# Last attention: GpSimd instead of VectorE multiplies the turned outputs by their reciprocal sums, and VectorE turns them back three heads later

## The chip, the cores and the metric

The kernel runs on one core of one Trainium2 chip. The metric is the device time of one execution, in microseconds. Engines: TensorE (PE; PEld its weight loads), VectorE (DVE), ScalarE (ACT), GpSimd (POOL), and SyncE (SP), which here only issues DMAs.

## What is computed

Four layers of attention and feed-forward blocks on 4096 tokens of 128 features. The change is in the attention of the last layer, which runs on B = 16 sequences of S = 256 tokens with 16 heads of 8 features:

```python
qkv = (x @ w_qkv.T + b_qkv).reshape(B, S, 3, H, hd)
q, k, v = (qkv[:, :, 0], qkv[:, :, 1], qkv[:, :, 2])
energy = jnp.linalg.norm(q, axis=-1)
mask = (energy > energy.mean() * SPARSITY_THRESHOLD).astype(x.dtype)
scores = jnp.einsum('bihd,bjhd->bijh', q, k) / jnp.sqrt(jnp.float32(hd))
scores = scores * mask[:, :, None, :]
probs = jax.nn.softmax(scores, axis=2)
context = jnp.einsum('bijh,bjhd->bihd', probs, v).reshape(B, S, D)
return context @ w_out.T + b_out
```

To this the expert outputs of the last feed-forward block and the residual are added.

## The kernel before

The whole model is one program with stages. The last stage is this attention; it handles the NB = 16 sequences one by one (called batches n below), each with 16 heads and S = 256 positions. Order within an engine is the order in which the code emits instructions; between engines, semaphores order the work. Every signal (`at_mx`, `at_rz` and so on) counts up and is waited for at a value.

For a batch, the steps are:

1. GpSimd splits q and k into three bf16 parts each (`build_pool`: ten dependent operations of 128x256), five batches ahead. SyncE writes the parts to a DRAM tensor `d_pt` (`parts_sp`, 2 DMAs) and loads them back as stacked rows (`set_sp`, 12 DMAs), four batches ahead.
2. TensorE forms scores (`score_pe`), two batches ahead, and VectorE reduces them to row maxima (`maxima_dve`, one reduction of 128x512 per head). Three PSUM banks hold scores, so TensorE is at most three heads ahead of VectorE.
3. GpSimd negates and splits the maxima (`maxparts_pool`), TensorE turns them (`maxrows_pe`), ScalarE copies them, SyncE sends them to the rows behind q (`maxrows_sp`).
4. TensorE forms the scores again, turned and less their maxima (`weights_pe`), ScalarE takes the exponential, TensorE multiplies with the values and a column of ones (`values_pe`, in groups of four heads), so that each head's sum stands beside its output, in PSUM bank 6, half a batch (8 heads) at a time.
5. Per half `hf`, VectorE turns this bank in blocks of 32x32 (`turned_dve`, 128x512), takes the reciprocals of the sums (`sums_dve`, 128x16) and multiplies the outputs with them (`normed_dve`, 128x128 into half of CX). When both halves are there, it turns CX back into CT (`back_dve`, 128x256).
6. TensorE applies `w_out` to CT and adds the gathered expert outputs (`out_pe`), VectorE adds bias and residual (`added_out_dve`), SyncE stores.

What order the engines keep in iteration n of the loops:

- VectorE (`attend_dve`): behind head h's reduction of batch n+2 stand: h = 4 `turned_dve` of (n-1, 1), h = 5 its `sums_dve`, h = 6 its `normed_dve`, h = 7 `back_dve` of n-1, h = 12 `turned_dve` of (n, 0), h = 13 its `sums_dve`, h = 14 its `normed_dve` and `added_out_dve` of n-1.
- TensorE (`attend_pe`): per head the weights of batch n and the scores of n+2; values every fourth head in two parts; at h = 5 `maxrows_pe` of n+1; at h = 12 `out_pe` of n-1, which waits for `back_dve` of n-1.
- GpSimd (`attend_pool`): `maxparts_pool` of n+1, which waits for all maxima of that batch, the copy of the values of n, two gathers, `build_pool` of n+5 while n+5 < 16.
- SyncE (`attend_sp`): `set_sp` of n+4, which waits until the parts have landed in DRAM, `parts_sp` of n+5, `maxrows_sp` of n+2, `store_sp` of n-1.

Most instructions are emitted in helpers, so that their line is the helper's: L204 matmul (`mm`), L217 tensor_tensor (`tt`), L221 tensor_scalar, L225 scalar_tensor_tensor, L231 reduction, L234 copy or cast. L2770 and L2789 are VectorE's turns, L2774 its reciprocal, L2602 `set_sp`, L2589 `parts_sp`, L2606 `maxrows_sp`, L2653 the gathers.

## Time and profile before

| | |
|---|---|
| median of 3 executions | 2154.72 us (2152.58 to 2161.21) |
| profiled execution | 2164.62 us, span 2162.3 us |
| mean granted clock of TensorE | 0.892 |

```profile
span 2162.3 us, 35614 instructions
## 1 busy us (share of the span) xinstructions
PE 1835.7 (85%) x12446; PEld 1206.0 (56%) x12446; DVE 1277.8 (59%) x4360; ACT 979.1 (45%) x2521; POOL 343.0 (16%) x582
## 2 busy tenths in 40 slices
PE   6888588888787999999998888987899854999888
PEld 5455455555555578874556666553544642963333
DVE  3687688888886445764333767160212332469986
ACT  2423466666665223334442332643453213537656
POOL 0000100000000002310000020004053034307642
PEclk9899699999997687989998568988899966979989
```

The first part gives each engine's busy time. The second cuts the span into 40 slices of 54 us; a digit is the busy share in tenths, and PEclk is the clock that TensorE was granted, in tenths of full speed (1.0 is 2.4 GHz, 0.5 is 1.2 GHz). The last attention fills the last four and a half slices.

### The profile page before, as it was taken

What the parts mean: (1) busy time and instruction counts of PE and PEld (TensorE: products, weight loads), DVE (VectorE), ACT (ScalarE), POOL (GpSimd) and SP (SyncE); (2) the same over time, 40 slices, a digit from 0 to 9 for tenths busy, and PEclk for the clock granted to TensorE, in tenths of its full rate; (3) what the DMA queues carried; (4) which work ended last, traced back from release to release, by engine and by line L of the source; (5) the groups of instructions that cost most, each with busy time, mean ns of one, the idle gap of its engine ahead of it and who ended that gap; (6) DMA issues with size and microseconds to landing.
All of it is one profiled execution on the core that took longest, in us unless ns stands there. A gap on an engine that the chain in (4) does not pass through costs nothing.

```text
span 2162.3 us, 35614 instructions
## 1 busy us (share of the span) xinstructions
PE 1835.7 (85%) x12446; PEld 1206.0 (56%) x12446; DVE 1277.8 (59%) x4360; ACT 979.1 (45%) x2521; POOL 343.0 (16%) x582
## 2 busy tenths in 40 slices
PE   6888588888787999999998888987899854999888
PEld 5455455555555578874556666553544642963333
DVE  3687688888886445764333767160212332469986
ACT  2423466666665223334442332643453213537656
POOL 0000100000000002310000020004053034307642
PEclk9899699999997687989998568988899966979989
DMA  3000200000000000000001100021023102606662
GB/s 116 1 13 13 51 26 27 26 22 25 26 27 35 0 1 2 3 2 0 1 0 79 42 1 1 1 88 36 6 22 56 78 24 71 115 25 101 104 103 39
DMA packets 93280, 76.10 MB, mean 35 GB/s; under 512 B 22320, under 2 KB 85168, under 8 KB 92336
## 3 DMA queue, kind: packets, MB, share of 16 engines
q1 hardware_dynamic: 85424, 65.31, 12.9%
q0 software_dynamic: 7680, 8.53, 2.2%
q8 instruction: 101, 1.65, 0.3%
q14 instruction: 75, 0.61, 0.1%
HBM read 48.86 MB, written 23.51 MB: 33 GB/s over the span
## 4 chain that ended last, share of the span: by engine, by line
PE 54%; DVE 27%; issue 6%; DMA 4%; SPq 3%; ACT 2%; another core or an unknown queue 1%; POOL 1%; DVEq 0%; PEld 0%; PEldq 0%; ACTq 0%; POOLq 0%
PE ps L204 50%; DVE sm L225 6%; DVE wt L225 5%; DVE big L217 3%; DMA d_pt<-big 3%; PE ps L208 2%; PE ps L2515 2%; SPq L2602 1%; DVE tmp L221 1%; DVE big L231 1%; SPq L909 1%; DVE big L225 1%; DVE sm L231 1%; DVE sm L221 1%
## 5 line engine op out<-in xcount | busy, mean ns | idle before, releaser
L213 ACT ACTIVATE tmp<-ps,bi 128x512 f32<-128x512 f32 (+1 forms) x226 | 153.6, 683 | 197.4 <-PE ps L204 183.6
L204 PE MATMUL ps<-big,mw 128*128 128x512 f32 (+3 forms) x476 | 217.9, 553 | 10.0 <-DVEq L252 5.6
L213 ACT ACTIVATE sm<-sm,wt 128x1 f32<-128x1 f32 x480 | 165.0, 344 | 78.8 <-DVE sm L225 50.7
L204 PE MATMUL ps<-big,co 128*128 128x256 f32 (+1 forms) x360 | 140.9, 509 | 62.8 <-ACT big L213 42.3
L213 ACT ACTIVATE big<-ps 128x512 f32<-128x512 f32 (+1 forms) x296 | 150.5, 558 | 77.4 <-PE ps L204 75.2
L231 DVE TENSOR_REDUCE big<-ps 128x2 f32<-128x512 f32 x256 | 160.5, 672 | 17.5 <-PE ps L204 16.5
L204 PEld LDWEIGHTS ps<-ke,big 32*128 32x128 f32 (+2 forms) x1632 | 126.6, 190 | 62.6 <-ACT big L212 46.4
L204 PE MATMUL ps<-ke,big 32*128 32x128 f32 (+2 forms) x1632 | 147.9, 291 | 13.1 <-ACT big L212 2.0
L204 PE MATMUL ps<-ke 48*128 48x256 bf16 (+4 forms) x638 | 126.1, 312 | 31.5 <-DVE big L217 15.4
L204 PE MATMUL ps<-big,tmp 128*32 128x256 f32 (+2 forms) x1180 | 123.5, 407 | 22.2 <-DVE tmp L221 16.7
L204 PE MATMUL ps<-tmp,mw 128*128 128x512 f32 x288 | 140.4, 599 | 0.7 <-ACT tmp L212 0.7
L212 ACT ACTIVATE big<-ps 128x256 f32<-128x256 f32 (+4 forms) x244 | 90.2, 379 | 105.3 <-PE ps L204 89.1
L204 PE MATMUL ps<-big 128*32 128x128 f32 (+5 forms) x898 | 128.5, 297 | 10.2 <-DVE big L231 4.4
L204 PEld LDWEIGHTS ps<-co,sm 128*128 128x128 f32 (+1 forms) x708 | 98.4, 213 | 63.9 <-DVE sm L333 38.4
L204 PE MATMUL ps<-big,wt 128*128 128x512 f32 x208 | 112.6, 644 | 22.3 <-DVEq L252 14.3
L204 PE MATMUL ps<-co,sm 128*128 128x128 f32 (+1 forms) x708 | 110.3, 307 | 23.2 <-DVE sm L333 14.1
L204 PEld LDWEIGHTS ps<-big,co 128*128 128x128 f32 x360 | 64.5, 203 | 93.8 <-ACT big L213 54.3
L204 PEld LDWEIGHTS ps<-big,mw 128*128 128x128 f32 (+1 forms) x476 | 80.8, 199 | 61.7 <-issue 37.3
L234 POOL COPY mw<-mw 128x64 f32<-128x64 f32 x64 | 16.4, 256 | 612.0 <-DMA mw<-d_tab 610.0
L204 PEld LDWEIGHTS ps<-ke 128*128 128x128 f32 (+3 forms) x638 | 64.4, 131 | 86.6 <-DVE big L217 24.2
L204 PE MATMUL ps<-tmp,wt 128*128 128x512 f32 (+1 forms) x212 | 102.0, 571 | 12.5 <-issue 7.8
L212 ACT ACTIVATE tmp<-ps 128x128 f32<-128x128 f32 (+2 forms) x177 | 61.9, 362 | 89.4 <-PE ps L204 52.7
(267 smaller groups left out, 3785.7 us busy)
## 6 DMA issues: line engine op xcount, KB each, us to landing
mw<-d_tab SPq DMA_DIRECT2D x32, 328.0 KB, 3.5
mw<-m SPq DMA_DIRECT2D x2, 4096.0 KB, 12.7
d_pt<-big SPq DMA_DIRECT2D x32, 192.0 KB
ke<-d_pt SPq DMA_DIRECT2D x72, 64.0 KB
big<-d_pt SPq DMA_DIRECT2D x72, 64.0 KB
mw<-d_pt SPq DMA_DIRECT2D x48, 64.0 KB
d_xs<-big SPq DMA_DIRECT2D x1, 2560.0 KB, 14.7
big<-d_xs SPq DMA_DIRECT2D x5, 512.0 KB, 6.4
```

What stands on the lines that cost most here:

```text
L204: return e.matmul(out, lhsT, rhs, start=start, stop=stop)
L208: return e.transpose(out, a, K("ident")[0:n, 0:n])
L212: return e.activation(out, in_, f, scale=scale, **kw)
L213: return e.activation(out, in_, f, bias=0.0 if bias is None else bias, scale=scale, **kw)
L217: return e.tensor_tensor(out, a, b, op)
L221: return e.tensor_scalar(out, a, s1, None, op0)
L225: return e.scalar_tensor_tensor(out=out, in0=a, scalar=s, in1=b, op0=op0, op1=op1)
L231: return e.tensor_reduce(out, a, AX, op)
L234: return e.tensor_copy(out, a)
L909: e.dma_start(BIG[2 + hh][q, :].rearrange("p (c x) -> p c x", x=256)[:, :, 64 * (b % 4):64 * (b % 4) + 64], EKT[q, 16 * hh:16 * hh + 16, : ...
L2515: p = e.matmul(o, TMP[:, 2 + i % 2, 128 * j:128 * j + 128], MW[:, bass.ds(x * 512 + (4096 + 128 * j), 128)], start=False, stop=(j == 3))
L2602: e.dma_start(st_[j][r0 + 8 * t:r0 + 8 * t + 8], d_pt[n, j, part].rearrange("(h d) n -> d h n", d=8)).then_inc(s_st[n % 4], 16)
```

## The change

The product of the turned outputs with the reciprocal sums is no longer formed by VectorE (`normed_dve`) but by GpSimd (`normed_pool`). In GpSimd's loop it stands behind `build_pool` of n+5: first the second half of batch n-1, then the first half of batch n; the second half of the last batch stands behind the loop. VectorE's `back_dve` moves from behind head 7 to behind head 10 and waits for GpSimd's products (`at_nm`). `turned_dve` waits for the product of the same half of the batch before, since it overwrites what that reads; `normed_pool` waits for the turn back of the batch before (`at_ct`), since it overwrites CX.

```diff
--- before.py
+++ after.py
@@ -2563,9 +2563,9 @@
         s_pw, s_mr = ([sem(f"d_{n_}{i}") for i in range(2)] for n_ in ("pw", "mr"))
         s_st, s_gy = ([sem(f"d_{n_}{i}") for i in range(4)] for n_ in ("st", "gy"))
         s_o = sem("d_o")
-        at_parts, at_v, at_m3 = signals("gpsimd", 32, 16, 16)
+        at_parts, at_v, at_m3, at_nm = signals("gpsimd", 32, 16, 16, 32)
         at_ms, at_mt, at_s, at_y, at_o = signals("tensor", 256, 16, 256, 128, 16)
-        at_mx, at_t, at_rz, at_ct, at_x, at_one = signals("vector", 256, 32, 48, 16, 16, 1)
+        at_mx, at_t, at_rz, at_ct, at_x, at_one = signals("vector", 256, 32, 32, 16, 16, 1)
         at_ex, at_m3c = signals("scalar", 256, 16)
         QROW = (0, 0, 0, 1, 1, 2)
         KROW = (0, 1, 2, 0, 1, 0)
@@ -2654,6 +2654,10 @@
                                          bass.IndirectOffsetOnAxis(ap=IXP[:, k:k + 1], axis=0)).then_inc(s_gy[n % 4], 16)
                 if n + 5 < NB:
                     build_pool(e, gn, n + 5)
+                if n:
+                    normed_pool(e, n - 1, 1)
+                normed_pool(e, n, 0)
+            normed_pool(e, NB - 1, 1)
 
 
         def mbank(m):
@@ -2767,6 +2771,8 @@
 
         def turned_dve(e, n, hf):
             e.wait_ge(*at_y(8 * n + 4 * hf + 4))
+            if n:
+                e.wait_ge(*at_nm(2 * n + hf - 1))
             e.transpose(TMP[:, hf, :], PS[:, 6, :]).then_inc(at_t.sem, 1)
 
         def sums_dve(e, n, hf):
@@ -2774,16 +2780,16 @@
             e.reciprocal(ZR[:, 16 * hf:16 * hf + 16].rearrange("p (x b) -> p x b", x=2),
                          TMP[:, hf, :].rearrange("p (x b d) -> p x b d", x=2, d=32)[:, :, :, 8]).then_inc(at_rz.sem, 1)
 
-        def normed_dve(e, n, hf):
-            e.wait_ge(*at_rz(3 * n + hf + 1))
-            p = tt(e, CX.rearrange("p (b x d) -> p x b d", x=4, d=8)[:, 2 * hf:2 * hf + 2],
-                   TMP[:, hf, :].rearrange("p (x b d) -> p x b d", x=2, d=32)[:, :, :, 0:8],
-                   ZR[:, 16 * hf:16 * hf + 16].rearrange("p (x b d) -> p x b d", x=2, d=1).broadcast_to((128, 2, 8, 8)), MU)
-            if hf:
-                p.then_inc(at_rz.sem, 1)
+        def normed_pool(e, n, hf):
+            if n:
+                e.wait_ge(*at_ct(n))
+            e.wait_ge(*at_rz(2 * n + hf + 1))
+            tt(e, CX.rearrange("p (b x d) -> p x b d", x=4, d=8)[:, 2 * hf:2 * hf + 2],
+               TMP[:, hf, :].rearrange("p (x b d) -> p x b d", x=2, d=32)[:, :, :, 0:8],
+               ZR[:, 16 * hf:16 * hf + 16].rearrange("p (x b d) -> p x b d", x=2, d=1).broadcast_to((128, 2, 8, 8)), MU).then_inc(at_nm.sem, 1)
 
         def back_dve(e, n):
-            e.wait_ge(*at_rz(3 * n + 3))
+            e.wait_ge(*at_nm(2 * n + 2))
             if n:
                 e.wait_ge(*at_o(n))
             e.transpose(CT, CX).then_inc(at_ct.sem, 1)
@@ -2806,21 +2812,16 @@
                         turned_dve(e, n, 0)
                     if h == 13:
                         sums_dve(e, n, 0)
-                    if h == 14:
-                        normed_dve(e, n, 0)
                     if h == 4 and n:
                         turned_dve(e, n - 1, 1)
                     if h == 5 and n:
                         sums_dve(e, n - 1, 1)
-                    if h == 6 and n:
-                        normed_dve(e, n - 1, 1)
-                    if h == 7 and n:
+                    if h == 10 and n:
                         back_dve(e, n - 1)
                     if h == 14 and n:
                         added_out_dve(e, n - 1)
             turned_dve(e, NB - 1, 1)
             sums_dve(e, NB - 1, 1)
-            normed_dve(e, NB - 1, 1)
             back_dve(e, NB - 1)
             added_out_dve(e, NB - 1)
```

## Rows read from the trace of the kernel before

**Rows 1.** Timeline of GpSimd, iteration 2: start us, length us, instructions, idle before and its releaser.

```profile
1967.71 0.29 POOL L221 TENSOR_SCALAR big<-big 128x32 f32<-128x32 f32 x1 [2.57 <-DVE big L231]
...
1977.56 0.40 POOL L234 CAST big<-big 128x256 bf16<-128x256 f32 x1
1980.47 0.29 POOL L221 TENSOR_SCALAR big<-big 128x32 f32<-128x32 f32 x1 [2.51 <-DVE big L231]
```

**Rows 2.** Table by stretch, from one start of `maxparts_pool` to the next.

```profile
1954.86:1967.71 12.85, 11.55 (x138) 4.84 (x138) 12.47 (x25) 9.23 (x19) 8.80 (x20) 1.00 0.60 92
1967.71:1980.47 12.76, 11.65 (x138) 4.90 (x137) 12.38 (x25) 8.90 (x19) 8.78 (x19) 1.00 0.66 106
2061.81:2078.87 17.06, 13.76 (x140) 5.53 (x140) 12.58 (x24) 8.88 (x17) 8.91 (x19) 0.80 0.60 92
2092.60:2109.60 17.00, 14.79 (x156) 5.95 (x158) 12.67 (x25) 9.86 (x19) 3.73 (x10) 0.80 0.59 109
2109.60:2122.18 12.58, 11.66 (x138) 4.91 (x140) 12.20 (x25) 8.90 (x18) 3.72 (x10) 1.00 0.51 69
2122.18:2134.75 12.57, 11.87 (x138) 5.20 (x142) 12.11 (x24) 8.78 (x18) 3.72 (x9) 1.00 0.09 24
```

**Rows 3.** Groups of GpSimd by line and shape, last attention: count, busy us, mean ns.

```profile
L217 POOL TENSOR_TENSOR big<-big 128x256 f32<-128x256 f32 x44 | 29.6, 673 | 3.5
...
L217 POOL TENSOR_TENSOR big<-big 128x32 f32<-128x32 f32 x32 | 7.8, 244 | 2.7
```

**Rows 4.** Timeline of VectorE, the same iteration.

```profile
1972.35 0.46 DVE L217 TENSOR_TENSOR tmp<-tmp,big 128x128 f32<-128x128 f32 x1
1972.74 0.68 DVE L231 TENSOR_REDUCE big<-ps 128x2 f32<-128x512 f32 x1
1973.34 0.43 DVE L2789 STREAM_TRANSPOSE tmp<-tmp 128x256 f32<-128x256 f32 x1
1973.69 3.04 DVE L231 TENSOR_REDUCE big<-ps 128x2 f32<-128x512 f32 x5
1976.66 0.69 DVE L2770 STREAM_TRANSPOSE tmp<-ps 128x512 f32<-128x512 f32 x1
1977.73 0.69 DVE L231 TENSOR_REDUCE big<-ps 128x2 f32<-128x512 f32 x1 [0.38 <-PE ps L204]
...
1979.04 0.27 DVE L217 TENSOR_TENSOR tmp<-tmp,big 128x128 f32<-128x128 f32 x1
1979.24 0.48 DVE L225 SCALAR_TENSOR_TENSOR big<-ps,bi,big 128x256 f32<-128x256 f32 x1
1979.63 1.87 DVE L231 TENSOR_REDUCE big<-ps 128x2 f32<-128x512 f32 x3
```

**Rows 5.** Timeline of TensorE, the same iteration: output product and the next weights.

```profile
1976.18 0.70 PE L204 MATMUL ps<-tmp,wt 128*128 128x256 f32 x2
...
1977.26 0.28 PE L204 MATMUL ps<-big 51*128 51x256 bf16 x1
```

**Rows 6.** Timeline of VectorE at the end of the kernel.

```profile
2157.61 0.29 DVE L217 TENSOR_TENSOR tmp<-tmp,big 128x128 f32<-128x128 f32 x1
2157.93 0.45 DVE L2789 STREAM_TRANSPOSE tmp<-tmp 128x256 f32<-128x256 f32 x1
```

**Rows 7.** Timeline of TensorE: the two longest waits for a transfer.

```profile
2063.30 0.39 PE L204 MATMUL ps<-big 51*128 51x256 bf16 x1 [3.30 <-DMA big<-big]
...
2094.10 0.39 PE L204 MATMUL ps<-mw 51*128 51x256 bf16 x1 [3.31 <-DMA mw<-big]
```

**Rows 8.** Table by stretch, TensorE alone: us, busy, clock, DMA share, GB/s.

```profile
2064.00:2066.00 2.00, 2.00 (x20) 0.50 0.65 88
```

**Rows 9.** SyncE: its longest total wait (us, times, longest), and issues of set loads.

```profile
SPq L2602 <- DMA d_pt<-big: 48.8, 11, 5.6
...
2047.34 4.64 SPq L2602 DMA_DIRECT2D mw<-d_pt  x12
...
2062.84 4.56 SPq L2602 DMA_DIRECT2D ke<-d_pt  x12
```

## The prediction

> **What bounds the kernel now.** I read the page first for the span, 2162.3 us, then the timeline of GpSimd for the rhythm of the last attention, because GpSimd's first negation of a batch (`maxparts_pool`) starts only when VectorE has finished a batch of row maxima, so each of its starts marks the start of a new iteration n [rows 1]. Call that start P(n). The table by iteration, cut at these starts, has P(1) = 1954.86, P(11) = 2092.60, P(12) = 2109.60 and P(14) = 2134.75 [rows 2]. Thirteen iterations therefore take 179.9 us of the 2162.3.
>
> The same table shows two regimes [rows 2]. In the undisturbed one an iteration takes 12.76 us and VectorE is busy for 12.38 of them; the last full iterations, in which GpSimd builds no parts any more, take 12.58. VectorE sets this pace: 16 reductions at 0.59 us, two turns, two reciprocals, two products, a turn back and a sum. In the other regime (the rows of 17.06 and 17.00 us) VectorE is busy for no more than 12.7 us, and the granted clock drops. The cause is in the timeline of TensorE: it stands for 3.30 us for the DMA of the maxima rows, and starts again at half clock, 0.50; a second stand of this kind, 3.31 us, opens the iteration at 2092.60 [rows 7, 8]. That DMA is queued on SyncE behind the loads and stores of the parts, and SyncE itself waits 48.8 us in 11 waits for the parts to land [rows 9]. So from P(6) or so to P(11) the chain of transfers and not VectorE sets the pace, while before P(6) and after P(12) it is VectorE.
>
> GpSimd is the relaxed engine. In one iteration its work runs from 1967.71 to 1977.96 (the start of its last cast plus 0.40), 10.25 us, and it then idles 2.51 us until the next batch of maxima [rows 1]. That 10.25 is the number on which the whole case turns, because the change hangs VectorE's turn back on what comes behind it.
>
> **The change part by part.**
>
> Removed from VectorE: two products of 128x128 per iteration. Their length is not what they cost, since neighbours overlap; I take start to start. The one at head 14 starts at 1979.04 and the sum after it at 1979.24, so 0.20. The one at head 6 starts at 1972.35, the reduction after it at 1972.74, so 0.39 while GpSimd works on its parts [rows 4]. Without GpSimd's parts an iteration is 12.58 instead of 12.76, so there I take 0.20 for each of the two, 0.39 together. The gain is 0.59 in an iteration with parts and 0.39 in one without, if nothing else is late.
>
> Added to GpSimd: two products of 128x128 behind `build_pool`. No row has this size; GpSimd's tensor_tensor takes 244 ns at 128x32 and 673 ns at 128x256 [rows 3]. A straight line gives 244 + 96 x (429/224) = 428 ns; I take 0.44, bounded by 0.24 and 0.67. The Trainium skill, GPSIMD Engine Reference, sections Instruction dispatch and Specifications, gives two-input operations a floor of about 2.5 cycles an element at 1.2 GHz, which is 0.27 us for 128 elements before start-up (an estimate from that page); no row here has it, and with 0.27 in place of 0.44 the sum below would fall by 1.7 us.
>
> Added waits. (a) `back_dve` of n-1, now after head 10, waits for `normed_pool` (n-1, 1). On GpSimd that product is behind the maxima parts, the values' copy, two gathers and the whole `build_pool(n+5)`. It starts at P + 10.25 + 0.08 (GpSimd's gap between dependent operations), ends at P + 10.77, and I allow 0.10 for the signal to VectorE (GpSimd to VectorE is not in the trace; VectorE to GpSimd is 0.15: the reduction of head 15 starts at 1979.63, takes 0.69 and so ends at 1980.32, and GpSimd starts at 1980.47 [rows 1, 4]; bounds 0 and 0.3). So VectorE turns back at P + 10.87. Without the wait it would be there much sooner: the reductions of heads 8 to 12 start at 1973.69 and take 2.97 us, so head 10 ends near P + 7.8, less 0.35 for the turn back that no longer stands ahead of it and 0.39 for the product: P + 7.1 [rows 4]. VectorE stands for 3.8 us. (b) Behind the turn back on VectorE are queued the reductions 11 to 15 of the next maxima, the turn (n, 0), its reciprocal and the sum of n-1. TensorE has to wait as well: `out_pe(n-1)` in its in-order stream at head 12 needs the turned outputs, and all its later scores and weights stand behind. ScalarE's exponentials follow TensorE. (c) `normed_pool` (n, 0) waits for that turn back and for the reciprocal of head 13; both come within 3.3 us after the turn back, well before the iteration's end, so the next `maxparts_pool` behind it is not delayed. (d) `turned_dve` waits for a product of the iteration before: long done.
>
> From the turn back to the next P, in pitches from start to start: turn back 0.35, heads 11 and 12 at 0.594 each 1.19, turn (n, 0) 0.69 (1.07 less the wait of 0.38), head 13 through reciprocal and head 14 to what follows 1.31 (1977.73 to 1979.04), the sum 0.39, head 15 up to GpSimd's next start 0.84. Together 4.77 us [rows 4]. Could TensorE be later? The output product starts at 1976.18 and the next pair at 1977.26, 1.08 us later [rows 5], and head 13's maxima began 1.55 after that start. It would start 0.48 after the turn back begins, so head 13's scores are ready at 2.03 and VectorE asks for them at 2.23: just in time at full clock.
>
> Iteration with parts, after: 10.87 + 4.77 = 15.64 us, a closed ring of GpSimd and VectorE, for n = 1 to 10. Before: 12.76 when undisturbed.
>
> The sum, against the profiled execution (span 2162.3, time 2164.62):
> - P(1) comes 0.20 sooner (product of head 14 of n = 0): 1954.66.
> - P(11) = 1954.66 + 10 x 15.64 = 2111.1, against 2092.60: +18.5. It is not 10 x 2.88, since before loses 10.1 us (137.7 less 127.6) of its own to the transfers up to there.
> - Iteration 11 took 17.00 because of the second wait for a transfer. After the change an iteration of 15.6 leaves the transfers time (a round of SyncE, from one set of loads to the next, took 15.5 us where they set the pace: 2047.34 to 2062.84 [rows 9]), so this wait goes: 12.58 - 0.39 = 12.19. +13.7 at P(12).
> - Iterations 12 and 13: -0.39 each. +12.9 at P(14).
> - The tail: turned, reciprocal, product, turn back is one chain there. The product starts 2157.61, the turn back 2157.93: 0.32 [rows 6]. On GpSimd the same costs a signal 0.15, 0.44 and a signal 0.10: 0.69. +0.35, so +13.2. The copy and gathers of batch 15 now stand behind the product (14, 0), about 5 us later than before, and are wanted 5 us or more after that.
> - The clock. TensorE reached the output product at P + 8.5 [rows 5] and would reach it up to 0.7 sooner; it gets it at P + 11.35. It stands 2.9 to 3.6 us in each of ten iterations. The trace has a stand of this length twice; 2 us behind the first the clock is 0.50 [rows 7, 8]. At 0.5 the output product takes 1.08 us more, of which 0.2 is hidden: 0.9 per iteration, 9 us for all ten. What the clock costs later in the iteration falls ahead of VectorE's wait and is free. But the clock need not fall each time, nor before the output product starts. I take it for four or five of ten: +4.
>
> Sum +17.2. On the profiled 2164.6 that is 2181.8; that execution was 9.9 us above the median of 2154.72, and I take the difference over to the median: 2172.
>
> **The rivals.**
> 1. Half clock every time. The Trainium skill, TensorE: Matmul & The Clock Gate, Why this matters for your kernels, says that a stand of TensorE sends it back to its lower clock; the first stand of 3.30 us agrees, with the clock at 0.50 behind it. By that rule alone all ten iterations pay 0.9. Worked out from the rows: 13.2 + 9 = +22, 2177; with GpSimd's product at its upper bound (0.23 more, ten times, and 0.2 of signal) 2181. For it: both stands of that length fell. Against: the lower end, 2.9 us, is shorter than either.
> 2. The transfers already cost as much (not slower by what can be told). The ring costs 15.64 us, and a round of SyncE 15.5. Had the median execution of before its transfers as pacemaker from P(2) on, instead of P(6), it would have lost up to 5 x 1.5 us more in this stage, so the cost would be 13.2 - 7.5 = +6: 2161. It decides from a round of 14.5 us in the early iterations. Against: the early ones are at 12.76 to 12.85 with VectorE full.
> 3. The wait of VectorE does not arise, if GpSimd is through its parts before head 10. It would need GpSimd's 10.25 us to be 7.1. VectorE gains 0.59 then, but the transfers take that back up to P(11); what is left is three times 0.39, less 0.35 in the tail: -1, 2154. If TensorE lost one half-clock phase by it, 2150. The row of 10.25 speaks plainly against it.
>
> **How the numbers follow.** Main case (ring of 15.6 us, half clock in some iterations) 0.55, 2166 to 2178. Rival 1: 0.21, 2177 to 2183. Rival 2: 0.14, 2160 to 2165. Rival 3: 0.07, 2150 to 2155. Something faster still: 0.03. About 0.5%, 10.8 us, is what a measurement of this kernel can tell from no change, so the line is at 2165.5. Slower: 0.77, which is the main case and rival 1 and a hundredth of the others. Within: 0.20. Faster: 0.03. The range of the unknown terms: product 0.24 and no signal -3, no half clock -4, gives 2165; product 0.67, signal 0.3 and half clock always gives 2181. Rival 2 is taken in: 2160 to 2181.
>
> **What would show it.** After the change GpSimd's starts should be 15.6 us apart for n = 1 to 10 and 12.2 for 11 to 13; VectorE's 128x256 turn should carry an idle time of over 3 us ended by GpSimd in ten iterations; TensorE's product of the turned outputs should carry a wait of about 3 us for VectorE; its 3.3 us waits for the DMA of the maxima rows should be gone. GpSimd's new product should be at 0.4 to 0.5 us. The forecast is wrong if GpSimd's starts stay at 12.8 us, if the waits for transfers stay although the ring is slower, or if the half clock stretches over the ring, which would make it longer than 16.5 us.

## The result and the profile after

The changed kernel takes 2183.28 us (median of 4 runs, 2181.77 to 2185.58), the kernel before in the same comparison 2157.23 (4 runs, 2152.58 to 2161.21). The ratio is 1.0122, 95% interval 1.0097 to 1.0148: slower by about 26 us. The forecast was slower too, but its 2172 was too low by 11 us, and the time lies 2.3 us above the top of the range, 2181.

From the page of the kernel after: span, busy time by engine, and TensorE's granted clock in 40 slices of the span, in tenths of full speed.

```profile
span 2180.1 us, 35665 instructions
...
PE 1852.3 (85%) x12446; PEld 1217.1 (56%) x12446; DVE 1270.5 (58%) x4328; ACT 979.1 (45%) x2521; POOL 356.7 (16%) x614
...
PEclk9998699999996688989997578988899767978889
```

The span was 2162.3 before, so it grew by 17.8. The last attention fills the last four and a half of the 40 slices, and no busy sum says where in it the time went. The table by stretch does. It is cut where [rows 2] is, at the starts of `maxparts_pool`: stretch and length, busy us of TensorE, its weight loads, VectorE, ScalarE and GpSimd (instructions in brackets), granted clock, DMA share, GB/s. These are iterations 1, 2 and 11, the tail (what lies behind P(14)), and iterations 1 to 10 together.

```profile
1951.47:1967.94 16.47, 12.82 (x130) 5.70 (x130) 11.87 (x23) 8.40 (x17) 9.63 (x21) 0.80 0.63 94
1967.94:1983.34 15.40, 13.58 (x152) 5.54 (x146) 12.16 (x23) 9.40 (x19) 9.64 (x22) 0.89 0.63 99
2112.97:2124.82 11.85, 11.43 (x138) 4.89 (x140) 11.80 (x23) 8.76 (x18) 4.57 (x12) 1.00 0.51 105
2148.63:2180.10 31.47, 21.95 (x222) 10.08 (x220) 7.63 (x16) 16.06 (x32) 8.07 (x17) 0.89 0.09 27
1951.47:2112.97 161.50, 130.24 (x1366) 56.74 (x1364) 120.28 (x221) 88.93 (x171) 96.33 (x210) 0.84 0.51 92
```

VectorE fills 11.8 to 12.2 us of an iteration here, as the change wanted (12.4 to 12.5 before), yet an iteration with parts takes 15.4 to 16.5 us instead of 12.76, and then no engine is full. Only from iteration 11 on does VectorE set the pace again. The same stretches in all profiles, in us, worked out from the starts of `maxparts_pool` and the span (the runs named e1 to e16 are told below):

```
                      P(1)->P(11)  P(11)->P(14)  P(14)->end   P(0)->end
before                  137.74        42.15        27.55        219.63
after                   161.50        35.66        31.47        240.86
e1_before_again         138.65        43.52        26.42        221.81
e2_move_only            137.98        39.58        27.34        217.10
e3_ahead                141.04        44.77        30.80        229.55
e4_warm                 153.74        35.55        30.75        232.99
e5_change_again         162.58        36.58        31.50        242.96
e6_tail                 163.34        37.53        37.01        250.21
e7_sp_before            138.08        37.80        28.18        216.26
e8_sp_ahead             145.53        37.93        36.09        232.50
e9_tail14               161.08        35.56        31.79        240.35
e10_half_before         127.80        37.69        26.37        205.08
e11_half_ahead          118.50        35.55        34.84        201.83
e12_ahead_tail14        135.60        41.75        31.78        222.07
e13_last                159.74        37.56        27.47        236.95
e14_ahead_last          136.99        43.05        27.42        219.60
e15_half_ahead_last     121.17        35.54        27.89        196.78
e16_longer              171.90        36.51        31.53        251.85
```

Now iteration 1 of the kernel after. First GpSimd (start us, length us, instruction, idle before it and its releaser), from behind `build_pool` on: the product (0, 1), the product (1, 0), the next maxima.

```profile
1961.84 0.41 POOL L217 TENSOR_TENSOR tmp<-tmp,big 128x128 f32<-128x128 f32 x1
1966.47 0.41 POOL L217 TENSOR_TENSOR tmp<-tmp,big 128x128 f32<-128x128 f32 x1 [4.22 <-DVE big L2780]
1967.94 0.29 POOL L221 TENSOR_SCALAR big<-big 128x32 f32<-128x32 f32 x1 [1.07 <-DVE big L231]
```

VectorE, same view and iteration, its turn back and its wait at head 13:

```profile
1962.28 0.45 DVE L2795 STREAM_TRANSPOSE tmp<-tmp 128x256 f32<-128x256 f32 x1 [3.62 <-POOL tmp L217]
...
1965.47 0.69 DVE L231 TENSOR_REDUCE big<-ps 128x2 f32<-128x512 f32 x1 [0.96 <-PE ps L204]
```

And TensorE, its output product, as in [rows 5]:

```profile
1962.78 1.22 PE L204 MATMUL ps<-tmp,wt 128*128 128x256 f32 x2 [3.40 <-DVE tmp L2795]
```

Read the three in order of time. GpSimd's product ends at 1962.25, the turn back starts at 1962.28 after 3.62 us of idleness, the output product at 1962.78 after 3.40 us in which TensorE stood (a stand, below, is such an idle stretch of TensorE). Then it takes 1.22 us, where [rows 5] has 0.70 for the same two matmuls: it runs at half clock (the rows further down), and the maxima of head 13 wait 0.96 us for TensorE (0.38 in [rows 4]). The waits of the stretch 1950 to 2112 (us in total, times, longest) say that this is the rule and not one iteration:

```profile
DVE tmp L2795 <- POOL tmp L217: 30.4, 10, 3.6
...
PE ps L204 <- DVE tmp L2795: 28.2, 10, 3.4
```

No wait of TensorE for a transfer is left in these ten iterations; the two of 3.3 us of [rows 7] are gone.

### The profile page after: what moved, and what is told of

Its sections match the earlier page's. It is cut to its first block, busy times and chain, and to the rows that moved or that the text cites. A ratio compares the mean times of both kernels' runs of the same rounds, so it can differ in the third digit from the quotient of the medians.

```text
span 2180.1 us, 35665 instructions
## 1 busy us (share of the span) xinstructions
PE 1852.3 (85%) x12446; PEld 1217.1 (56%) x12446; DVE 1270.5 (58%) x4328; ACT 979.1 (45%) x2521; POOL 356.7 (16%) x614
## 3 DMA queue, kind: packets, MB, share of 16 engines
q1 hardware_dynamic: 85424, 65.31, 12.4%
## 4 chain that ended last, share of the span: by engine, by line
PE 56%; DVE 27%; POOL 5%; issue 5%; ACT 2%; another core or an unknown queue 2%; SPq 1%; DMA 1%; DVEq 0%; PEld 0%; PEldq 0%; ACTq 0%; POOLq 0%
PE ps L204 52%; DVE sm L225 6%; DVE wt L225 5%; DVE big L217 3%; PE ps L208 2%; PE ps L2515 2%; DVE big L231 2%; POOL big L217 1%; POOL big L234 1%; DVE tmp L221 1%; SPq L909 1%; DVE big L225 1%; POOL mw L2653 1%; DVE sm L231 1%
## 5 line engine op out<-in xcount | busy, mean ns | idle before, releaser
L231 DVE TENSOR_REDUCE big<-ps 128x2 f32<-128x512 f32 x256 | 159.5, 673 | 12.7 <-PE ps L204 12.4
L204 PE MATMUL ps<-tmp,wt 128*128 128x512 f32 (+1 forms) x212 | 106.7, 595 | 38.3 <-DVE tmp L2795 30.4
L234 POOL COPY mw<-mw 128x64 f32<-128x64 f32 x64 | 16.5, 258 | 609.7 <-DMA mw<-d_tab 607.7
## 6 DMA issues: line engine op xcount, KB each, us to landing
mw<-m SPq DMA_DIRECT2D x2, 4096.0 KB, 12.5
```

The costliest lines, as they stand in the source:

```text
L204: return e.matmul(out, lhsT, rhs, start=start, stop=stop)
L231: return e.tensor_reduce(out, a, AX, op)
L234: return e.tensor_copy(out, a)
```

## The experiments

The runs came in four groups, each with its own runs of before. The kernel before has medians of 2118.5, 2162.85, 2119.01 and 2158.92 us in them. In the profiles that difference lies ahead of the last attention (P(0) at 1904.59 against 1942.67). So only ratios to before within a group and stage times are compared; each stage time is that of one profiled execution. A ratio stands with its 95% interval, and the number behind it, where there is one, is P(1) to P(11) in us.

### Where does the time come from: the move, the product's place, or the clock?

My theory after reading this profile was that the place of the product behind `build_pool` closes the ring and the half clock comes on top. The rivals: the later turn back costs by itself, or a product on GpSimd is dear wherever it stands.

**Before once more, one execution**, for the spread between executions.

> The kernel before once more, for a second profiled execution. The profiled one of before lay 7.4 us above its median of 2157.2, and the forecast carried its difference over. If that excess sits in the last attention (transfers late by chance), P(1) to P(11) takes clearly less than 137.7 us here, say 131 to 135, and a time near 2157. If it sits ahead of the last attention, P(1) to P(11) is 137 to 139 again.

Measured: 2128.24 us. P(1) to P(11) took 138.65, the tail 26.42. TensorE's waits for transfers fell in other iterations than in the first profile of before, and the stage, P(0) to the end, took 221.81 where it had taken 219.63. So the excess of a profiled execution over its median is not in these ten iterations.

**The turn back three heads later, and nothing else** (before with this edit):

```
-                    if h == 7 and n:
+                    if h == 10 and n:
                         back_dve(e, n - 1)
```

> Only the turn back is moved, from behind head 7 to behind head 10; the products stay on VectorE. My theory (VectorE's wait for a product behind GpSimd's parts is the cost, not the later turn back): as before within 0.3%, 2151 to 2163, iterations of 12.8 us where VectorE paces. Rival (the later turn back holds TensorE's output product at head 12 and with it all scores): iterations of 14 us or more and 2168 or more.

Measured: ratio 1.0012 [0.9992, 1.0031], ten iterations in 137.98. The place of the turn back costs nothing. An undisturbed iteration even falls from 12.76 to 12.45, and the wait of 0.38 in [rows 4] goes. The order on TensorE is as it was. But TensorE's scores of head 12 wait for VectorE's reduction of head 9 (three banks), and the turn back no longer stands ahead of that one: the output product starts at P + 8.16 (1933.22 less 1925.06) instead of P + 8.47, and head 13's maxima find their scores ready.

**The product (n-1, 1) ahead of `build_pool`** (the change with this edit):

```
+                if n:
+                    normed_pool(e, n - 1, 1)
                 if n + 5 < NB:
                     build_pool(e, gn, n + 5)
-                if n:
-                    normed_pool(e, n - 1, 1)
                 normed_pool(e, n, 0)
```

> The changed kernel with GpSimd's product of the second half (n-1, 1) ahead of build_pool(n+5) and not behind it. Nothing else is changed. Theory: GpSimd then forms it near P + 5.0 and VectorE's turn back at P + 7.2 does not wait; GpSimd's starts are 12.2 us apart where VectorE paces and 12.8 to 17 where the transfers do; TensorE's 3 us waits for the turn back are gone in iterations 1 to 10; 2153 to 2162, the tail's 3.5 us included. Rival (products on GpSimd cost by their signals or by taking turns with VectorE at SBUF, wherever they stand): iterations stay above 14 us and the time above 2170.

Measured: ratio 1.0028 [1.0007, 1.0048]. GpSimd's timeline of this kernel: one batch of maxima, the product inside the iteration, the next batch.

```profile
1932.84 0.29 POOL L221 TENSOR_SCALAR big<-big 128x32 f32<-128x32 f32 x1 [0.72 <-DVE big L231]
...
1937.40 0.41 POOL L217 TENSOR_TENSOR tmp<-tmp,big 128x128 f32<-128x128 f32 x1
...
1944.69 0.29 POOL L221 TENSOR_SCALAR big<-big 128x32 f32<-128x32 f32 x1 [0.74 <-DVE big L231]
```

The product is done at P + 4.97 and not at P + 10.78, the turn back has no wait, and this iteration takes 11.85 us. So the place closes the ring, not GpSimd's product as such. But ten iterations take 141.04 and not 118.5. TensorE's waits in that kernel's last attention:

```profile
PE ps L204 <- DMA mw<-big: 10.9, 3, 4.7
PE ps L204 <- DMA ke<-big: 9.3, 3, 3.4
...
PE ps L204 <- DMA big<-big: 6.2, 3, 3.2
```

26.4 us are waits for transfers, 11.8 in the profile of before and 17.6 in its repetition. Taken up again below.

**TensorE kept at work in the stand** (the change with unread matmuls ahead of the wait in `out_pe`):

```
+            if n < 10:
+                for _ in range(8):
+                    mm(e, PS[:, 5, 256:512], W("w3o"), W("qkv", 0, 256))
             e.wait_ge(*at_ct(n + 1))
```

> The changed kernel with eight matmuls of 128x256 fp32 whose result nobody reads ahead of each output product of batches 0 to 9, to fill TensorE's stand of 3.4 us. Theory (the step from 15.4 to 16.5 us per iteration is the half clock behind the stand): the granted clock stays at 1.00 from P(1) to P(11), all ten iterations take 15.4 us, and the time falls by 7 us to 2176. Rival (the step has another cause, such as transfers or PSUM waits): iterations stay at 16.5 us in most cases, 2183 or more. If the added matmuls run over the stand, an iteration is longer by what they overrun.

Measured: ratio 1.0091 [1.0064, 1.0117]. Its table by stretch (iteration 1 and the ten together), then its turn back on VectorE:

```profile
1913.16:1928.54 15.38, 15.04 (x160) 8.21 (x162) 11.78 (x23) 9.21 (x19) 9.61 (x21) 1.00 0.64 104
...
1913.16:2066.90 153.74, 148.52 (x1528) 79.17 (x1530) 117.83 (x221) 89.25 (x172) 96.05 (x211) 1.00 0.54 99
```

```profile
1923.95 0.45 DVE L2798 STREAM_TRANSPOSE tmp<-tmp 128x256 f32<-128x256 f32 x1 [3.60 <-POOL tmp L217]
```

The clock is 1.00 in every iteration and each takes 15.36 to 15.38, while VectorE still waits 3.60. This is the bare ring. The change's 161.50 less ten of 15.38 leaves 7.7 us for the clock: six iterations pay 1.07 to 1.09, two pay 0.41 and 0.75, and two (15.40 each) nothing. TensorE's output product in the kernel after, iterations 2, 3, 6 and 7, which took 15.40, 15.79, 16.45 and 16.13 (iteration 10 is as 2, with a stand of 1.72 and 15.40):

```profile
1979.25 0.70 PE L204 MATMUL ps<-tmp,wt 128*128 128x256 f32 x2 [1.72 <-DVE tmp L2795]
...
1994.64 0.70 PE L204 MATMUL ps<-tmp,wt 128*128 128x256 f32 x2 [3.40 <-DVE tmp L2795]
...
2043.37 1.22 PE L204 MATMUL ps<-tmp,wt 128*128 128x256 f32 x2 [2.42 <-DVE tmp L2795]
...
2059.84 0.88 PE L204 MATMUL ps<-tmp,wt 128*128 128x256 f32 x2 [3.41 <-DVE tmp L2795]
```

The full price, a product of 1.22 us, is paid behind stands of 3.40 and also of 2.42; a stand of 3.40 leaves the product at 0.70 once and at 0.88 another time; both stands of 1.72 cost nothing. So the length of the stand alone does not say which iteration pays. The granted clock in the kernel after does, in the table by stretch (iterations 1 and 2, then 3):

```profile
1961.50:1962.50 1.00, 0.00 (x0) 0.00 (x0) 0.22 (x1) 0.00 (x0) 0.67 (x2) 0.50 0.60 57
1966.00:1971.00 5.00, 5.00 (x44) 1.49 (x40) 4.12 (x9) 3.18 (x7) 2.95 (x9) 0.50 0.71 81
1972.00:1979.00 7.00, 5.53 (x74) 2.06 (x66) 5.07 (x10) 4.68 (x10) 5.99 (x12) 1.00 0.52 107
...
1994.00:1995.00 1.00, 0.36 (x2) 0.34 (x3) 0.86 (x2) 0.00 (x0) 0.11 (x1) 1.00 0.68 91
1995.50:1998.50 3.00, 3.00 (x25) 1.31 (x26) 2.71 (x7) 1.57 (x3) 0.41 (x1) 0.50 0.78 128
```

In iteration 1 the clock is down in the stand, before the product starts at 1962.78: full price. In iteration 3 it is still 1.00 when the product starts at 1994.64 and 0.50 just behind it: part of the price. In iteration 2 it does not fall, and the stand is short because TensorE comes to it late: it was at half clock for more than the first 3 us of this iteration. What decides when the clock falls no run here shows.

**GpSimd a little longer** (the change with two copies of 128x256 behind `build_pool`, one execution):

```
                     build_pool(e, gn, n + 5)
+                    for r in range(2):
+                        cp(e, RES, QF3[:, 0:S]).then_inc(gv, 1); e.wait_ge(gv, gn.up())
```

> The changed kernel with two more copies of 128x256 on GpSimd (nobody reads them) between build_pool and the product (n-1, 1), 0.94 us together. Theory (iterations 1 to 10 are a closed ring of GpSimd and VectorE): each of them grows by 0.94 us, to 16.3 at full clock and 17.4 with the output product at half clock, P(1) to P(11) from 161.5 to 170 or 172; iterations 11 to 13 stay at 11.85. Rival (something else has become the bound): less than half of that.

GpSimd's timeline of this kernel, iteration 1:

```profile
1952.26 0.29 POOL L221 TENSOR_SCALAR big<-big 128x32 f32<-128x32 f32 x1 [0.19 <-DVE big L231]
...
1962.61 0.87 POOL L234 COPY big<-big 128x256 f32<-128x256 f32 x2
1963.56 0.41 POOL L217 TENSOR_TENSOR tmp<-tmp,big 128x128 f32<-128x128 f32 x1
...
1969.66 0.29 POOL L221 TENSOR_SCALAR big<-big 128x32 f32<-128x32 f32 x1 [1.06 <-DVE big L231]
```

Eight iterations take 17.40 and two 16.34, where the change has 16.46 and 15.40: the 0.94 us added on GpSimd (0.87 and a gap of 0.07) came out as 0.94 in each kind. The ten together grew by 10.4 us, 1 us more than ten times that, since eight of them and not six paid the full price of the clock. The engine that was idle 2.5 us of each iteration before now sets its length.

### Was the first profile typical, and what does the tail cost?

**The change again.** No edit.

> The changed kernel once more, beside the others of this group. On the first chip it cost 26 us, while its last attention, from P(0) to the end, took 21.2 us more than in the profiled execution of before (240.9 against 219.6). If the change costs what it costs in this stage alone, it is 18 to 22 us slower than before here and the stage again takes 239 to 242 us. If 26 us is right, something outside the stage or the spread of before adds 5.

Measured: ratio 1.0106 [1.007, 1.0143]; 162.58 and a tail of 31.50. The medians are 23 us apart and the stage took 242.96, each 1 us above what was expected. In the tail, 3.9 us longer than before where 0.35 was predicted, I first suspected the order of the last batches.

**The product (n-1, 1) earlier, for n = 14 and 15**:

```
+                if n > 13:
+                    normed_pool(e, n - 1, 1)
...
-                if n:
+                if 0 < n < 14:
                     normed_pool(e, n - 1, 1)
```

> The changed kernel, with the product (n-1, 1) ahead of the copy and the gathers in iterations 14 and 15 alone. Theory (the 3.9 us that the changed kernel's tail lost come from VectorE's turn back of batch 13 waiting 2.4 us behind GpSimd's copy and two gathers, since in these iterations no reductions fill the time): P(14) to the end falls from 31.5 to 28 us, the time by 3.5 us against the changed kernel. Rival (the tail lost it to the signals on its chain, 0.35 per product): no more than 1 us falls.

Measured: ratio 1.015 [1.0113, 1.0186], and the tail grew to 37.01. TensorE's timeline there, and a stretch of the table behind it:

```profile
2169.56 0.64 PE L204 MATMUL ps<-big,tmp 128*32 128x256 f32 x8 [1.30 <-POOL tmp L234]
...
2172.00:2181.00 9.00, 9.00 (x62) 4.04 (x57) 1.45 (x3) 3.20 (x7) 0.41 (x1) 0.50 0.08 24
```

Now the values' copy of batch 15 stands behind a product that comes late, and TensorE waits for that copy. I had repaired one wait by making another. The wait of 1.30 us is the smaller part of the 5.5: from 2 us behind it TensorE is busy without a pause at half clock, 0.50, for 9 us and more. In the kernel after the clock falls in the tail only behind the last values.

**The same for n = 14 alone**:

```
+                if n == 14:
+                    normed_pool(e, n - 1, 1)
...
-                if n:
+                if n and n != 14:
                     normed_pool(e, n - 1, 1)
```

> The changed kernel with the product (13, 1) ahead of the copy and the gathers in iteration 14 alone; e6_tail had it so in iteration 15 too, where the copy of the last values then stood behind a product whose reciprocal comes late, and lost 5.5 us. Theory: in iteration 14 the wait of the turn back for this product shrinks from 2.4 to 0.6 us as it did in e6_tail, iteration 15 is as in the changed kernel, and P(14) to the end goes from 31.5 to 29 or 28. Rival (nothing gained, because TensorE paces the last two batches): 31 or more.

Measured: ratio 1.0157 [1.0119, 1.0195] from four runs, one of them 10 us above the others; tail 31.79. No gain, so the order was not the cause. The cause shows in the end of the kernel after (VectorE, GpSimd and the store's issue):

```profile
2171.21 0.41 POOL L217 TENSOR_TENSOR tmp<-tmp,big 128x128 f32<-128x128 f32 x1 [3.72 <-DVE big L2780]
2171.65 0.45 DVE L2795 STREAM_TRANSPOSE tmp<-tmp 128x256 f32<-128x256 f32 x1 [0.58 <-POOL tmp L217]
2173.61 0.48 DVE L225 SCALAR_TENSOR_TENSOR big<-ps,bi,big 128x256 f32<-128x256 f32 x1 [1.51 <-PE ps L204]
2174.12 0.33 SPq L2610 DMA_DIRECT2D outT<-big  x1
```

VectorE's last sum ends at 2174.09 and the span at 2180.1, 6.0 us later. In before, its repetition and e2_move_only this is 2.2 us. So the span's end waits for something other than VectorE's sum and its store. My suspicion fell on GpSimd: its last product ends at 2171.62, 8.5 us before the span's end.

**The last product alone back on VectorE** (the product (15, 1), behind its reciprocal):

```
-            normed_pool(e, NB - 1, 1)
...
+        def last_dve(e):
+            n, hf = NB - 1, 1
+            e.wait_ge(*at_ct(n))
+            e.wait_ge(*at_rz(2 * n + hf + 1))
+            tt(e, CX.rearrange("p (b x d) -> p x b d", x=4, d=8)[:, 2 * hf:2 * hf + 2],
...
+            e.wait_ge(*at_rz(33))
+
         def back_dve(e, n):
-            e.wait_ge(*at_nm(2 * n + 2))
+            e.wait_ge(*at_nm(2 * n + (2 if n < NB - 1 else 1)))
...
             sums_dve(e, NB - 1, 1)
+            last_dve(e)
             back_dve(e, NB - 1)
```

> The changed kernel with one product less on GpSimd: the very last, (15, 1), is formed by VectorE again. Theory (GpSimd needs 8.3 us after its last instruction before the program can end; in before its last instruction lies 20 us ahead of the end, in the changed kernel 2.5 us ahead of the last store): GpSimd's last product is now (15, 0), 4.1 us earlier, the span ends 2.2 us behind VectorE's last sum as in before and no longer 6.0 us, and P(14) to the end falls from 31.5 to 27.3. Rival (the tail is lost by the waits for GpSimd's products in iterations 14 and 15): with one such wait less 0.4 us falls and no more.

Measured: ratio 1.0099 [1.0071, 1.0128]. VectorE's last sum in this kernel, as above:

```profile
2174.56 0.48 DVE L225 SCALAR_TENSOR_TENSOR big<-ps,bi,big 128x256 f32<-128x256 f32 x1 [1.55 <-PE ps L204]
```

The sum ends at 2175.04 and the span at 2177.2: 2.2 us again, and the tail is 27.47. Against the kernel after, the tail is 4.0 us shorter by one product on another engine, while the sum ends 25.3 us behind P(14) here and 25.5 there: that is the missing 3.6 us, with some spread. The ratio alone could not have told it, since its interval overlaps those of the change.

### Why does the product ahead of `build_pool` bring nothing?

Theory: an iteration of 11.85 us asks more of the transfers than they give. Rival: SyncE's order (set loads, which wait for parts to land, ahead of the next parts' stores) holds them up.

**SyncE's order exchanged, on the kernel before**:

```
-                if n + 4 < NB:
-                    set_sp(e, n + 4)
                 if n + 5 < NB:
                     parts_sp(e, n + 5)
+                if n + 4 < NB:
+                    set_sp(e, n + 4)
```

> The kernel before with two lines of SyncE's loop exchanged: parts_sp(n+5) ahead of set_sp(n+4). Nothing is changed on the other engines. Theory (a round of transfers is long because SyncE waits, before each set of loads, for parts that are queued behind the set before): the parts then land beside the loads, TensorE's waits for transfers go from 16 us to under 5 us, iterations stay at 12.8, P(1) to P(11) falls from 138 to 129 and the time by 8 to 12 us. Rival (the 14 to 15 us of a round are the transfers' own length): no change, within 3 us.

Measured: ratio 0.9993 [0.9974, 1.0012], 138.08, as the rival had it.

**The same exchange with the product ahead of `build_pool`** (and with the edit of e6_tail):

> Products on GpSimd with those of the second half ahead of the parts (as e3_ahead) and ahead of the copy in the last two iterations (as e6_tail), and SyncE's loop as in e7_sp_before. If VectorE paces once the transfers no longer do, its 0.6 to 0.9 us per iteration now counts: iterations of 11.9 us, P(1) to P(11) 119 to 124, and 8 us below e7_sp_before. If the transfers still pace, both are alike within 3 us, and taking work off VectorE is worth nothing here.

Measured: ratio 1.005 [1.0026, 1.0073], 145.53. Neither expectation came true: it is 13 us above e7_sp_before and not 8 below or within 3. About 8 of the 13 are the tail (36.09), which the edit of e6_tail explains, with the half clock as there; 7 are in the ten iterations. The order of issue is not what holds the transfers.

**Half of the set loads left out from batch 6 on, on the kernel before.** Part of the scores is then computed from stale rows:

```
-                for t, part in enumerate(parts):
+                for t, part in enumerate(parts if n < 6 else parts[:3]):
```

> The kernel before with half of the loads of parts left out: from batch 6 on, set_sp loads the first three of the six row blocks of q and k, so the other rows keep an earlier batch's parts and the scores of these batches are not the reference's. All other work is unchanged. Theory (the transfers pace before from P(6) or so on): TensorE's waits for transfers vanish, iterations are 12.8 throughout, P(1) to P(11) is 128 and P(11) to P(14) 38, and the time 12 to 15 us below before. Rival (the long iterations have another cause): P(1) to P(11) stays above 135.

**The same with the product ahead of `build_pool`** (and the edit of e9_tail14):

> The same half of the loads left out, in the changed kernel with the second half's product ahead of build_pool and of the copy in iteration 14. With the transfers out of the way and no wait for GpSimd, what the change takes off VectorE must count: iterations of 11.85 us, P(1) to P(11) 118.5, P(11) to P(14) 35.6; 9 to 12 us below e10_half_before. Rival (the work moved off VectorE is worth nothing even then, since TensorE paces at 12.7): within 3 us of e10_half_before.

**And that kernel with all its loads:**

> All loads, products on GpSimd with the second half's ahead of build_pool, and ahead of the copy in iteration 14. The best form of this change I know. Theory: transfers pace P(1) to P(11) at 138 to 142 as in e3_ahead, P(11) to P(14) is shorter than before's by 0 to 2, and the tail is 28 to 29: the time within 0.3% of before, and 18 to 22 us below the changed kernel. Rival: it beats before by more than 6 us, if the transfers held e3_ahead back only by chance.

Measured, ratios to before with all loads: e10_half_before 0.9957 [0.9938, 0.9975], e11_half_ahead 0.995 [0.9925, 0.9976], e12_ahead_tail14 1.0039 [1.0011, 1.0066]. The ten iterations came out as expected in the first two, the times did not: e10_half_before is 8 or 9 us below before and not 12 to 15, and e11_half_ahead only 3 us below e10_half_before (2107.39 against 2110.66) and not 9 to 12, since its tail is 8.5 us longer. e12_ahead_tail14 missed its tail of 28 to 29. With half of the loads gone ten iterations take 127.80 with the product on VectorE and 118.50 with it on GpSimd: 0.93 us an iteration. That is the 0.59 that the prediction took for the two products, and the 0.33 that e2_move_only found for the wait at head 13 (12.78 less 12.45). With all loads it is 137.74 or 138.65 against 135.60 to 141.04. The tail of e11_half_ahead, 34.84, is 3 us longer than that of e12_ahead_tail14 with the same code there. It is the clock once more. The same 6 us of both tails, 4.8 us behind P(14), e11_half_ahead first:

```profile
2078.00:2084.00 6.00, 6.00 (x36) 2.42 (x29) 0.97 (x2) 2.66 (x5) 1.01 (x2) 0.50 0.17 48
```

```profile
2096.90:2102.90 6.00, 6.00 (x64) 2.90 (x57) 1.46 (x3) 4.48 (x9) 2.70 (x4) 1.00 0.25 69
```

TensorE is busy all the time in both and gets through 36 matmuls in one and 64 in the other. Both had stood 0.98 us for the values' copy just before; in one the clock fell and in the other it did not.

**Both repairs together**, the edit of e3_ahead and that of e13_last:

> As e3_ahead (the second half's products ahead of build_pool), with the last product on VectorE as in e13_last. The best form after both findings. The transfers still pace P(1) to P(11), 135 to 142; the tail is 27. About 4 us below e3_ahead and e12_ahead_tail14 in ratio, so 0.999 to 1.002 of before: no gain that can be told. Rival: under 0.997, a version that beats before.

**And with half of the set loads:**

> e14_ahead_last with half of the loads of parts left out from batch 6 on (as e10_half_before; the scores of these batches are not the reference's). With the transfers and GpSimd's end out of the way all that VectorE saves must reach the time: P(1) to P(11) 118.5, P(11) to P(14) 35.6, tail 27: P(0) to the end 194 against 205.1 in e10_half_before, so 11 us below it. Rival: the end is again later than 2.2 us behind the last sum, and the gain is 3 to 4 us as in e11_half_ahead.

Measured: ratios 1.0000 [0.9979, 1.002] and 0.9914 [0.9892, 0.9935]. The stage of e15_half_ahead_last is 8.3 us below that of e10_half_before, not 11: its first four iterations took 12.2 to 13.5 and not 11.85, and its tail 27.89 against 26.37. The ten iterations of e10_half_before and of e15_half_ahead_last in the table by stretch:

```profile
1917.64:2045.44 127.80, 115.31 (x1366) 48.13 (x1363) 124.03 (x241) 89.49 (x172) 87.99 (x190) 1.00 0.48 92
```

```profile
1951.90:2073.07 121.17, 114.50 (x1366) 48.94 (x1364) 118.68 (x221) 88.21 (x171) 95.85 (x210) 1.00 0.51 97
```

And those of e14_ahead_last, with all loads:

```profile
1955.74:2092.73 136.99, 119.19 (x1346) 50.29 (x1342) 120.46 (x220) 88.36 (x169) 95.45 (x211) 0.91 0.64 102
```

In the first two VectorE is busy for 97 to 98% of the stretch, in the third for 88%: with half of the loads it is the bound, and then the relief counts. With all loads the best version of the change equals the kernel before, and no version with all loads beats it. Two things stay open. Leaving loads out takes away bytes and DMAs together, so it does not say which of them paces. And the clock is 1.00 in the first two stretches but 0.91 in the third, so what the transfers take back there are their waits and the half clock that comes with them; no run parts the two.

## Why the prediction was right and wrong

**In short.** The time is 11.3 us above the forecast. Of these, 4.0 are the stage's, which cost 21.2 us where the sum had 17.2: the step on the clock was 3.7 too low and the step on the tail 3.6, the ring 2.6 too high and iterations 11 to 13 0.9. The other 7.3 came with the last step, which carried the sum over to the median: 2.5 because the median of before moved from 2154.72 to 2157.23 with a fourth run, 4.8 because the medians differ by more than the stage. With the errors of the stage alone the forecast would have been 2176, inside the range; it is this last step that put the time outside, and its cause stays open.

**The ring: right in mechanism, 0.26 us too long.** Every link was where it was put. GpSimd's product took 0.41 (0.44 predicted) and began at P + 10.37 (10.33), the turn back began at P + 10.81 (10.87), and the signal from GpSimd to VectorE took 0.03, where 0.10 was allowed. From the turn back to the next P it was 4.59 in the undisturbed clock of e4_warm (4.77). Hence 15.38 instead of 15.64, and 2.6 us less over ten iterations. e3_ahead shows that the place of the product closes the ring, e16_longer that GpSimd is in it with its full length, e2_move_only that the later turn back has no part in it.

**The clock: right in mechanism, taken at half its size.** The step that failed is "I take it for four or five of ten". I took +4 for four or five of ten; it was 7.7 in eight of ten. Against rival 1 I had said that a stand of 2.9 us is shorter than either of [rows 7]. Two examples bound nothing: the row of 2.42 above pays in full. The Trainium skill, TensorE: Matmul & The Clock Gate, Why this matters for your kernels, says that a gap between bursts of matmuls, if it is long enough, sends TensorE back to its lower clock, and rival 1 priced a fall in each iteration at 9; the trace agrees with that page in eight iterations of ten. e4_warm takes the whole cost away. The price of one is 1.08, which is what I had for the lengthening before I took 0.2 of slack off; VectorE's wait of 0.96 at head 13 is most of it, and there is none in e4_warm.

**Iterations 11 to 13: right in mechanism, 0.9 us too long in all.** They take 11.89 on average instead of 12.19. I left the wait of 0.38 at head 13 in them [rows 4], though the step for (b) had taken that very wait out of the iterations with parts. e2_move_only shows it going with the turn back alone. The second wait for a transfer of [rows 7] went as predicted.

**The tail: wrong.** +3.9 instead of +0.35. The chain of turn, reciprocal, product and turn back was costed well, even a little too dear: VectorE's last sum ends 25.46 us behind P(14) (2174.09 less 2148.63) and 25.34 in before, +0.12. The other 3.80 lie behind the sum. What failed is the step that took the end of this chain as the end of the program, and so put the end of GpSimd's work at nothing. The trace of before could not show it, since GpSimd's last instruction there ends 20 us before the end.

**The sum.** In the last attention the four terms predicted -0.2, +22.7, -5.6 and +0.35, together +17.2. Measured are +0.04, +23.8, -6.5 and +3.9, together +21.2. The errors of the ring and the clock nearly cancelled inside the second term (-2.6 and +3.7), which is luck, so of the four terms the tail is missed by most. Against the profiled execution, the sum named 2181.8 and the changed kernel's profiled execution took 2181.95. That agreement is chance: P(0) was 3.4 us earlier there, ahead of anything that the change touches.

**Carrying it over to the median: wrong, and the cause stays open.** The medians differ by 26 us, 5 more than the stage. The repetition gives 23 (2185.92 less 2162.85) with a stage of 242.96. The kernel before spreads over 9 us in four runs and over 19 in seventeen, so with four runs these 5 us can be spread. I can't show that they are, and it stays open. Taking the profiled execution's 9.9 us above the median off the forecast was correct arithmetic, but the profiles of after do not carry such an excess, and the range, built from terms of this stage alone, had no room for it.

**The rivals.** Rival 2 (transfers already as dear) fell as a forecast of the change: before has 138 us in both profiles, of which 10 are the transfers', as the sum had it and as e10_half_before shows (127.80). Its mechanism, transfers that set the pace, is real, though, and decides in e3_ahead, e12_ahead_tail14 and e14_ahead_last. Rival 3, the wait that does not arise, is what e14_ahead_last makes of the change by another place of one call: it foresaw that the transfers would take the gain up to P(11), and the ratio is 1.0000.

## What to carry to other kernels

An engine that idles 2.5 us in 12.8 does not have 2.5 us to give at any place: ask when the moved step can run at the earliest, behind everything that is queued on that engine, and when its reader wants it. If the reader's engine then sets when the first engine may begin its next round, the two make a ring, and its length is the sum of both halves. Before relieving the engine that fills its rounds, look for what comes late next in the same stretch (here the loads, visible in the slow iterations of the trace), since it takes the gain back. And ask of an engine that gets the last work of a kernel what its end costs; here the span went on 8.5 us behind GpSimd's last product.

## What the hardware showed that I had not expected

**The end of GpSimd's work.** In all ten kernels whose last product is GpSimd's, the span ends 8.45 to 8.54 us behind the end of that product (2171.62 and 2180.1 in the kernel after), while VectorE's last sum ends anywhere from 5.5 to 6.4 us before it. In the three with the last product on VectorE, GpSimd's last one ends 8.6, 8.6 and 9.0 us before the span's end, and the sum 2.2 us before it, as in before. So these three are just about free of it. What GpSimd does in these 8.5 us no run shows.

**The length of a stand does not tell its price.** Behind TensorE's stands of 2.42 to 3.41 us the output product took 0.70, 0.88 or 1.22 us, as the clock fell behind its start or before it. Behind a stand of 0.98 us the clock fell in e11_half_ahead and made the tail 3 us longer, and did not fall in e12_ahead_tail14. And eight unread matmuls in the stand kept the clock at 1.00 and gave 7.7 us back. Needless work in a waiting engine can shorten what comes behind the wait.

**Signals between engines are short.** GpSimd's product ended at 1962.25 and VectorE started on it at 1962.28.
